# Slot one-hots written plain by VectorE and scaled twice by ScalarE; the tile-to-expert tables in two parts at the first and third tile of the one-hots

## The reference, cut to what matters

```python
probs = jax.nn.softmax(xt @ Wr.T + bias, axis=-1)
topk_val, topk_idx = jax.lax.top_k(probs, 2)
w = topk_val / (jnp.sum(topk_val, axis=-1, keepdims=True) + EPS)
...
oh = jax.nn.one_hot(topk_idx, 16, dtype=x.dtype)
routed = jnp.einsum('tke,tk,teh->th', oh, w, y)
shared = jax.nn.silu(xt @ sWg) * (xt @ sWu) @ sWd
return (routed + shared).reshape(b, s, h)
```

## Time and profile before

| what | value |
|---|---|
| median of 3 runs | 1061.99 us (1059.1 to 1067.91) |
| the profiled execution's own time | 1064.05 us |
| its span, first to last instruction | 1062.3 us |
| TensorE busy | 970.4 us, 91% |
| VectorE busy | 555.0 us, 52% |
| ScalarE busy | 487.5 us, 46% |
| GpSimd busy | 299.4 us, 28% |

### The profile page before, as it was taken

The page is one execution under the profiler, slowest core; times in us unless marked ns, Lnnn a source line. Parts: engine busy times, 40 slices in busy tenths (PEclk is TensorE's granted clock), DMA queues, the critical chain, the costliest instruction groups (busy, mean ns, idle before and its releaser), DMA issues.

```text
span 1062.3 us, 20312 instructions
## 1 busy us (share of the span) xinstructions
PE 970.4 (91%) x6623; PEld 650.5 (61%) x6623; DVE 555.0 (52%) x1652; ACT 487.5 (46%) x1163; POOL 299.4 (28%) x320
## 2 busy tenths in 40 slices
PE   6668699999999999999998899899899999799994
PEld 5333468686776868686776687778644444344441
DVE  8875257575666657565667677578511111111110
ACT  7212177777767777777778422211122222222221
POOL 2276120111102020111111046333323643354432
PEclk9689899999999999999999999899999999999997
DMA  6133733250624334240533111711368757955443
GB/s 210 39 94 91 171 81 87 73 111 1 136 56 89 72 81 97 69 105 6 131 124 103 62 70 58 277 51 40 109 206 271 146 86 216 286 96 103 88 70 40
DMA packets 44564, 114.31 MB, mean 108 GB/s; under 512 B 9332, under 2 KB 11380, under 8 KB 42162
## 3 DMA queue, kind: packets, MB, share of 16 engines
q1 hardware_dynamic: 32146, 87.14, 28.7%
q0 software_dynamic: 12320, 25.90, 12.9%
HBM read 53.03 MB, written 25.17 MB: 74 GB/s over the span
## 4 chain that ended last, share of the span: by engine, by line
PE 71%; DVE 7%; issue 7%; DMA 6%; POOL 4%; ACT 3%; SPq 1%; POOLq 0%; ACTq 0%; DVEq 0%
PE psum L1258 11%; PE psum L518 11%; PE psum L488 8%; PE psum L531 7%; PE psum L508 7%; DMA w_dn<-in_wd 6%; PE psum L1339 6%; PE psum L493 5%; PE psum L1202 4%; PE psum L1186 3%; PE psum L1279 2%; PE psum L534 2%; PE psum L1301 1%; POOL hot_all L1423 1%; DVE oh_lo L1498 1%
## 5 line engine op out<-in xcount | busy, mean ns | idle before, releaser
L642 DVE CUSTOM_DVE_ANT_0 psum<-psum,mask_row 128x128 f32<-128x128 f32 (+7 forms) x256 | 194.3, 762 | 58.1 <-PE psum L508 55.7
L600 ACT ACTIVATE probs<-psum,nmax 128x128 f32<-128x128 f32 (+7 forms) x256 | 190.4, 744 | 47.4 <-DVE nmax L642 42.7
L1258 PE MATMUL psum<-attnT,x_T 128*128 x376 | 177.5, 594 | 8.2 <-SPq L748 6.9
L518 PE MATMUL psum<-ident,probs 128*128 128x128 f32 x1152 | 173.9, 276 | 4.7 <-ACT probsT L585 3.2
L508 PE MATMUL psum<-k_stack,q_stack 128*128 128x512 f32 (+2 forms) x384 | 155.5, 460 | 16.9 <-issue 8.8
L518 PEld LDWEIGHTS psum<-ident,probs 128*128 128x128 f32 x1152 | 136.9, 141 | 37.0 <-issue 18.9
L1159 DVE COPY x_T<-psum 128x512 f32<-128x512 f32 x47 | 32.5, 691 | 223.8 <-PE psum L1301 223.8
L585 ACT COPY probsT<-psum 128x512 f32<-128x512 f32 (+3 forms) x256 | 129.1, 504 | 37.8 <-PE psum L518 33.0
L488 PE MATMUL psum<-xnT,w_unit 128*128 128x512 f32 x256 | 130.5, 599 | 0.2 <-ACT full L463 0.2
L435 POOL CAST part_hi<-full 128x512 fp32r<-128x512 f32 x32 | 19.6, 612 | 350.7 <-ACT full L463 246.0
L859 POOL DMA_INDIRECT out<-xnT,slot_out x47 | 74.5, 1584 | 150.9 <-DMA out<-xnT,slot_out 104.6
(11 more groups left out here) (223 smaller groups left out, 1405.8 us busy)
## 6 DMA issues: line engine op xcount, KB each, us to landing
attnT<-in_wgu SPq DMA_DIRECT2D x16, 1024.0 KB, 5.4
q_stack<-part_hi SPq DMA_DIRECT2D x64, 128.0 KB, 2.4
q_stack<-part_lo SPq DMA_DIRECT2D x64, 128.0 KB, 2.4
k_stack<-part_hi SPq DMA_DIRECT2D x64, 128.0 KB, 2.4
k_stack<-part_lo SPq DMA_DIRECT2D x64, 128.0 KB, 2.4
w_dn<-in_wd SPq DMA_DIRECT2D x16, 512.0 KB, 6.1
out<-acc SPq DMA_DIRECT2D x17, 256.0 KB, 2.3
hot_all<-xn SPq DMA_DIRECT2D x4, 1024.0 KB, 8.0
```

The source lines that it names most:

```text
L518: mm = pe.transpose(bank(4 + m % 2)[:, (j - 4 * k) * P:(j - 4 * k + 1) * P], probs[n % PSLOTS][:, j * P:(j + 1) * P], ident[:, :])
L600: act.activation(probs[n % PSLOTS][:, 0:(i + 1) * P], bank(2 * (n % 2), 2)[:, 0:(i + 1) * P], ACT.Exp, bias=nmax[:, n % 4:n % 4 + 1], scal ...
L642: dve.tensor_tensor_reduce(out=row, in0=row, in1=mask_row[:, (QT - 1 - i) * P:QT * P], scale=1.0, scalar=3.0e38, op0=ALU.add, op1=ALU.min, ...
L1258: mm = pe.matmul(bank(2 + p), lhs(k), rhs(k), start=(k == 0), stop=(k == KC - 1), skip_group_check=True)
```

## The change

VectorE writes the tile one-hot once, without a factor, to a new ring `slot_one`; ScalarE copies it twice with a scale, into the two halves of `slot_hi`. VectorE so issues two instructions for a group of choices where it issued three, and ScalarE issues two where it issued none. ScalarE does this in `slot_values`, at the end of its own iteration n, behind `silu(n)` and ahead of `turn_high(n)`. TensorE's `slots` waits for `slot_lo` and for the two scaled copies. `tile_experts` is cut in two: the first two of its instructions (`experts_of_tiles`) go to VectorE's iteration 6 and the other eight (`first_tiles`) to iteration 8, each ahead of the one-hots of that iteration; iteration 13 is left with none of it.

```diff
+            def slot_values(n0, n1):
+                for n in range(n0, n1):
+                    c, k, r = n // TOPK, n % TOPK, n % SLOT_RING
+                    act.wait_ge(s_slot1, n + 1)
+                    if n >= SLOT_RING:
+                        act.wait_ge(s_slotm, n - SLOT_RING + 1)
+                    for part, value in ((0, tok_no1[:, c:c + 1]), (1, w_top[:, c, k:k + 1])):
+                        act.activation(slot_hi[:, r, part, :], slot_one[:, r, :], ACT.Copy,
+                                       scale=value).then_inc(s_slotv, 1)
+
             for n in range(SHARED):
                 if n >= 1:
                     turn_high(n - 1)
                 silu(n, n % 2)
+                if SLOT0 <= n < SLOT0 + 7:
+                    slot_values(5 * (n - SLOT0), min(5 * (n - SLOT0) + 5, TOPK * NT))
...
-            def tile_experts():
+            def experts_of_tiles():
                 je = [P, TILES, E]
...
+            def first_tiles():
+                je = [P, TILES, E]
...
                     dve.tensor_scalar(slot_lo[:, r, :], iota_f[:, :], pos_hlf[:, 1, k, c:c + 1], None,
                                       ALU.is_equal).then_inc(s_slot, 1)
-                    dve.tensor_scalar(slot_hi[:, r, 0, :], iota_j[:, :], pos_hlf[:, 0, k, c:c + 1],
-                                      tok_no1[:, c:c + 1], ALU.is_equal, ALU.mult).then_inc(s_slot, 1)
-                    dve.tensor_scalar(slot_hi[:, r, 1, :], iota_j[:, :], pos_hlf[:, 0, k, c:c + 1],
-                                      w_top[:, c, k:k + 1], ALU.is_equal, ALU.mult).then_inc(s_slot, 1)
+                    if n >= SLOT_RING:
+                        dve.wait_ge(s_slotv, 2 * (n - SLOT_RING + 1))
+                    dve.tensor_scalar(slot_one[:, r, :], iota_j[:, :], pos_hlf[:, 0, k, c:c + 1], None,
+                                      ALU.is_equal).then_inc(s_slot1, 1)
...
-                if n == SLOT0 + 7:
-                    tile_experts()
+                if n == SLOT0:
+                    experts_of_tiles()
+                if n == SLOT0 + 2:
+                    first_tiles()
                 if SLOT0 <= n < SLOT0 + 7:
                     slot_onehots(5 * (n - SLOT0), min(5 * (n - SLOT0) + 5, TOPK * NT))
...
             def slots(n0, n1):
                 for n in range(n0, n1):
-                    pe.wait_ge(s_slot, 3 * n + 3)
+                    pe.wait_ge(s_slot, n + 1)
+                    pe.wait_ge(s_slotv, 2 * n + 2)
```

More of the change, by code:

```diff
@@ L238, in build @@
         slot_hi = sb("slot_hi", [P, SLOT_RING, 2, TILES])
+        slot_one = sb("slot_one", [P, SLOT_RING, TILES])
         slot_f = sb("slot_f", [P, TILES])
@@ L280, in build @@
         s_slot = sem("slot_onehots_ready")
+        s_slot1 = sem("slot_tile_onehots_ready")
+        s_slotv = sem("slot_tile_values_ready")
         s_slotm = sem("slot_matmuls_done")
```

## The result

The changed kernel takes 1072.22 us in the median of 12 runs (1068.17 to 1077.36), the kernel before beside it 1062.41 us (12 runs, 1059.1 to 1067.91). The ratio is 1.0086, with a 95% interval of 1.0069 to 1.0102: slower by 9.8 us, 0.9%. The profiled execution took 1074.46 us, its span is 1072.7 us.

The account below looks back on a forecast made before the run. TensorE, busy 91% of the span, was taken as the bound. Terms -3.1 (tile 13), +2.8 + 1.2 (tile 6), +0.4 (copies), +4.4 + 1.2 (tile 8) gave +6.9 us on 1061.99: 1068.9, rounded 1069.0; range 1061.5 to 1074.

Parts of the forecast that it names:

- Iteration 6: Down of tile 6 starts 2.8 us later: first part of the tables, two added holds under GpSimd's splits, copies before `gs_hi`.
- Iteration 8: Down of tile 8 comes 4.4 us later through the second part of the tables and new holds; 3.2 without those holds.
- The half clock: TensorE at 1.2 instead of 2.4 GHz behind the waits before downs 6 and 8: +1.2 us each, or 0.
- the gain of iteration 13: Without the tables `gs_lo` of tile 13 is in time: 4.1 us go, 3.1 net of the gather.
- The gather: First routed rows, next late after tile 13: 5.2 us needed from `slot_tokens`, 4.2 left, so 1.0 us comes back.
- The copies: ScalarE's ten scaled copies, 0.226 us each, before `gs_hi`: some 0.1 us in tiles 7 and 9 to 12, 0.4 in all.
- ScalarE is the bound: Rival: copies at 0.290 us or more make ScalarE the bound in every tile; +11.4 us, 1073.4; chance 0.12.
- Milder: Rival: the holds don't add up and the clock holds; +1 to +3 us, 1063 to 1065; chance 0.27.
- Not slower: Rival: holds vanish at `gs_lo` of tiles 6 and 8, adding only 0.9 and 2.6; -0.6 us, 1061.4; chance 0.08.
- Made up later: Rival: the time lost is made up in the routed stage, where TensorE waits for weights; 0, 1062; chance 0.08.

Follow-up runs that it names:

- fewer splits: The change with GpSimd's `xs_lo` of tiles 9 and 11 left out; single run, only its trace read: waits of 3.24 and 3.57 us before downs 6 and 8.
- tokens early: The change with `slot_tokens` made in iteration 13 instead of 14; ratio 1.0066 to the kernel before.
- tokens late: The change with the ten table instructions spread behind the one-hots of iterations 7 to 12, `slot_tokens` staying in iteration 14; ratio 1.0005 to the kernel before.
- spread tables: The change with the ten table instructions spread behind the one-hots of iterations 7 to 12 and `slot_tokens` in iteration 13; ratio 0.9961 to the kernel before.
- late copies: The change with ScalarE's scaled copies one iteration later, behind the next `gs_hi`; 1067.51 us in a single run.
- copies alone: The change with the whole of the tables put back to iteration 13, so only the one-hots differ from the kernel before; ratio 1.0000 to it.
- three groups in the first tile: The spread tables version with three groups of one-hots in iteration 6 instead of five, four in iteration 12; ratio 0.9951 to the kernel before.
- first part alone: The change with the second part of the tables put back to iteration 13, the first staying in iteration 6; ratio 1.0021 to the kernel before.
- tables alone: The kernel before with only the tables moved, to iterations 6 and 8, all one-hots on VectorE; ratio 1.0085 to the kernel before.

## Why the prediction was right, and where its terms were off

The direction, the places and the mechanism were as put; 1069.0 was forecast, and 1072.22 lies within the range. The range owes some of that to luck: the forecast's own band (1066 to 1072) ends just below, and what took the range up to 1074 was a price of the copies that didn't come about. One per cent was also called about what a measurement can tell; with twelve runs of each kernel the interval of the ratio is 0.33% wide, and a loss of 0.9% is plain. By its steps:

- **Iteration 6, +2.8 predicted, +2.68 measured.** The holds fell on one-hots as worked out, at 713.01 and 713.71. Without the long one the wait is 0.84 us shorter (fewer splits); with the copies behind `gs_hi`, 1.1 us shorter. These two were varied one by one; the rest of the wait was not. What was held was `slot_one` in the fourth pair, not `slot_lo`, and behind the split's end (714.92) four copies still had to run before `gs_hi`.
- **Iteration 8, +4.4 predicted, +4.45 measured**, by the same reading.
- **The half clock, +1.2 twice predicted, 1.6 twice measured.** The term was taken from the six matmuls of down 13 alone. Here it reaches past them into the slot multiplications (1.99 for 1.04 us) and the next gate-up. Even before the change it went 0.24 us further than I counted (down 13 to 14 took 5.80 us and takes 4.33 now: 1.47, not 1.23), which is most of why the gain of iteration 13 is 4.5 instead of 4.1; the rest, 0.17, is that down 12 to 13 got 2.99 us shorter and not only by the wait's 2.82.
- **The gather, +1.0 predicted, +1.84 measured.** `slot_tokens` to the first issue took 2.0 us, as read. The landing was read off the queue's bytes at 3.2 us behind the issue; the chain shows 3.84, and 0.14 to TensorE. This is the mis-sized piece.
- **The clock behind the gather, not predicted, +1.7.** I gave the wait its length and asked nothing of the clock behind it, although TensorE then also waits for the copies of the turned rows (1.09 us). Two runs show it: gone with the tokens early, there again with the tokens late on top of the spread tables. It is the largest of the missing terms, and the least certain: with the late copies a wait of 1.55 us for the gather had the full clock behind it.
- **The copies, +0.4 predicted, 0 measured.** Ten in a row start 0.22 to 0.24 us apart, 0.227 in the mean (tile 11, 749.34 to 751.38), against 0.226 predicted. ScalarE: Activation LUTs of the Trainium skill, section What ACT_TABLE_LOAD costs, gives 186 ns and 0.833 ns a column, 93 more for a scale read from memory and 93 less when back to back, for 47 columns an estimate of 0.225 us: the trace agrees. What I had too long was the way to the first copy: 0.33 us from the start of the one-hot, where it is 0.27 (749.07 to 749.34). That is most of the 0.07 us by which `gs_lo` was to be late: it starts 5.00 us behind `silu` (746.99 to 751.99) and not 5.07, and 5.00 before the change. VectorE's pair is shorter too, 0.35 us (712.11 to 712.46) and not 0.42, but behind the first copy ScalarE's 0.45 a pair is the slower.

The terms that were short add up to 0.8 (clock) + 0.8 (gather) + 1.7 (clock behind it), the ones on the other side (copies and iteration 6 put too high, iteration 13's gain put too low) to 0.4, 0.1 and 0.4: 6.9 + 3.3 - 0.9 = 9.3, the stretch's 9.4. The median moved by 9.8, so 6.9 forecast 70% of it.

Of the rivals, "ScalarE is the bound" would have given a similar time (1073.4) for another reason; the copies alone, at a ratio of 1.0000, rule it out. "Milder" needed the clock to hold and the holds not to add up: neither happened. "Not slower" needed the holds to vanish: the comparison took 1.53 us under its split, where it took 1.52 in iteration 13 before, and the two new ones came on top. "Made up later" falls with the routed stage, which began 9.4 us later and made none of it up (the span is 10.4 us longer). GPSIMD Engine Reference of the Trainium skill, section Key points, says that GpSimd shares its SBUF interfaces with VectorE and contends with its two-port modes and with instructions of two SBUF inputs. For two inputs the trace agrees: the comparison took 1.53 us for 0.94. `slot_one` has one tensor input and was held too, 1.24 for 0.24 us; in which mode an instruction ran no row shows.

What stays open: what decides whether a wait of 1.5 to 3 us is followed by the half clock (below), whether spread tables make the waits for routed weights longer, and how the wait before down 8 divides between the length of the second part and the rest, since that part wasn't shortened by itself in its new place.

## What to carry to other kernels

Work taken from an engine that isn't the bound is worth only what the bound engine waits for it: ask what stands between the moved work and the next instruction that releases the bound engine, and put the moved block behind that instruction or in pieces that fit the idle time before it. When a wait goes, price what is next late to its landing, not to its issue, and add the clock behind each new wait of the bound engine. An edit that is worth nothing alone, as the copies here, can be worth something once other work is put in the room that it makes: 2.6 us of the stretch here, though the ratios (0.9961 with them, 0.9982 without) have overlapping intervals.

## What the runs showed of the hardware that I had not expected

- The granted clock behind a wait doesn't follow from the wait's length alone. One wait is the same in all twelve kernels, since the code up to it is the same: 1.99 to 2.01 us before the first transposes of the shared expert (679.32 before). In five traces (before, the change, copies alone, tokens early, late copies) the 2.5 us behind it have a granted clock of 0.50 to 0.63, in the other seven 1.00. Elsewhere the clock was at 2.4 GHz behind waits of 1.00, 1.39, 2.20 and 2.42 (both for routed weights; fewer splits, three groups in the first tile) and 2.95 us (late copies). It fell to 1.2 GHz behind 2.00, 2.25 and 2.44 (routed weights; first part alone, tables alone, tokens late), behind 2.58 and 2.82 for `gs_lo`, and behind all nine waits for `gs_lo` of over 3 us. Waits for the gather of 1.56 (tables alone), 1.68, 1.74 (fewer splits) and 2.32 us, each with 1.0 to 1.1 us more before the next gate-up, were followed by 1.2 GHz, one of 1.55 us (late copies) with 1.1 us more was not. Between shared downs a stretch at half clock cost 1.5 to 2.6 us here. So in a single trace a difference of that size, behind a wait of 1.5 to 3 us, need not come from the edit.
- A hold under GpSimd isn't a share of the work but a wait for the split's end: the `slot_one` issued at 713.71 ends at 714.95, 0.03 us behind `xs_lo`; the comparison, with 752 elements to handle, ends 0.79 us behind its `xs_lo` (709.57 + 1.53 = 711.10 against 709.01 + 1.30 = 710.31) and takes 0.94 where no split runs. So all but 0.15 to 0.21 us of the held instruction's own time comes behind the split. Instructions with an input in PSUM weren't held: `gated` took 0.42 us beside an `xs_hi` and 0.41 elsewhere, the addition to `acc` 0.68 us both beside an `xs_lo` and elsewhere.
